# Graph attention with layer norm: empty rows found by DVE, additions and low parts moved to ACT and POOL, scores ahead of values, one store of turned weights

## The reference

```python
q, k, v = heads(x @ Wq.T), heads(x @ Wk.T), heads(x @ Wv.T)
a = einsum('bhnd,bhmd->bhnm', q, k) * 512 ** -0.5 + (adj + adj)[:, None]
row_nonzero = any(a != 0, axis=-1, keepdims=True)
a = where(row_nonzero, a, -inf)
p = softmax(a); p = where(isnan(p), 0.0, p)
o = einsum('bhnm,bhmd->bhnd', p, v)
out = layernorm(x + merge(o) @ Wo.T)
```

## Time and profile before

| | us |
|---|---|
| median of 3 runs | 2044.13 (2043.81 to 2044.32) |
| the profiled execution's own time | 2047.55 |
| its span | 2045.7 |
| PE busy | 1801.1 (88%) |
| DVE busy | 1605.2 (78%) |
| POOL busy | 1509.2 (74%) |
| ACT busy | 1228.8 (60%) |
| transfers of the SP queue | 378.61 MB, 69.5% of 16 DMA engines' span |

### The profile page before, as it was taken

The page is one execution under the profiler, slowest core; times in us unless marked ns, Lnnn a source line. Parts: engine busy times, 40 slices in busy tenths (PEclk is TensorE's granted clock), DMA queues, the critical chain, the costliest instruction groups (busy, mean ns, idle before and its releaser), DMA issues.

```text
span 2045.7 us, 46740 instructions
## 1 busy us (share of the span) xinstructions
PE 1801.1 (88%) x14370; PEld 1452.7 (71%) x14370; DVE 1605.2 (78%) x6191; ACT 1228.8 (60%) x4886; POOL 1509.2 (74%) x2292
## 2 busy tenths in 40 slices
PE   7798988989888999889889889898898989898886
PEld 5676777777776777767767777676776777777764
DVE  4887878878777878878878788787777887887786
ACT  5566566656655665566566656665665566556554
POOL 4567777777777777777777777777777777777765
PEclk9998998989999999999999899899998999999999
DMA  4667767777776677677767767777777777767664
GB/s 163 177 181 198 190 181 197 187 186 197 186 192 187 182 195 190 188 200 187 188 189 197 190 187 188 195 187 183 190 187 195 186 193 192 188 185 206 174 174 144
DMA packets 269290, 382.63 MB, mean 187 GB/s; under 512 B 19056, under 2 KB 149104, under 8 KB 268912
## 3 DMA queue, kind: packets, MB, share of 16 engines
q1 hardware_dynamic: 268464, 378.61, 69.5%
q10 hardware_dynamic: 576, 1.05, 0.1%
HBM read 212.86 MB, written 166.72 MB: 186 GB/s over the span
## 4 chain that ended last, share of the span: by engine, by line
POOL 43%; DMA 19%; DVE 15%; issue 10%; PE 7%; SPq 3%; ACT 1%; DVEq 0%; POOLq 0%; ACTq 0%
POOL is_zero L357 24%; DMA e_t<-blocks 15%; DVE neg_a L822 6%; POOL folded_once L360 4%; POOL xt_lo L347 4%; DVE e_sb L860 4%; DMA blocks<-e_b 3%; PE ps_s L535 3%; PE ps_o L553 3%; POOL folded_twice L362 3%; SPq L292 2%; POOL folded L367 2%; POOL ln_tmp L398 2%; DVE e_b L870 2%; DVE x_sb L798 1%
## 5 line engine op out<-in xcount | busy, mean ns | idle before, releaser
L690 ACT ACTIVATE e_sb<-neg_a,neg_max 128x128 f32<-128x128 f32 x2048 | 792.4, 392 | 71.3 <-DVE neg_max L822 70.9
L357 POOL TENSOR_SCALAR is_zero<-neg_a 128x1024 uint8<-128x1024 f32 x256 | 711.0, 2777 | 158.6 <-DVE neg_max L822 137.5
L676 ACT ACTIVATE x_sb<-x_sb,shift,rstd 128x512 f32<-128x512 f32 x124 | 100.9, 815 | 708.0 <-POOL shift L406 703.8
L822 DVE CUSTOM_DVE_ANT_0 neg_a<-ps_s,adj_sb 128x128 f32<-128x128 f32 x2048 | 441.7, 285 | 76.3 <-PE ps_s L535 76.3
L471 PE MATMUL ps_w<-xt_hi,w_lo 128*128 128x512 f32 x1020 | 426.6, 418 | 0.0
L472 PE MATMUL ps_w<-xt_lo,w_hi 128*128 128x512 f32 x1020 | 407.2, 399 | 0.0
L690 ACT ACTIVATION_READ_ACCUMULATOR e_sb<-neg_a,neg_max 128x1 f32 x2048 | 391.5, 191 | 0.0
L553 PE MATMUL ps_o<-e_t,v_sb 128*32 128x128 f32 x4080 | 167.3, 314 | 214.1 <-DMA e_t<-blocks 214.1
L870 DVE STREAM_TRANSPOSE e_b<-e_sb 128x1024 f32<-128x1024 f32 x254 | 316.3, 1245 | 27.0 <-DVE e_sb L860 0.5
L860 DVE SCALAR_TENSOR_TENSOR e_sb<-e_sb,r_inv 128x1024 f32<-128x1024 f32 x256 | 313.7, 1225 | 9.1 <-DVE r_inv L857 0.4
L553 PEld LDWEIGHTS ps_o<-e_t,v_sb 128*32 128x32 f32 x4080 | 128.0, 124 | 262.8 <-issue 261.2
(11 more groups left out here) (103 smaller groups left out, 2793.7 us busy)
## 6 DMA issues: line engine op xcount, KB each, us to landing
blocks<-e_b SPq DMA_DIRECT2D x254, 512.0 KB, 3.3
e_t<-blocks SPq DMA_DIRECT2D x508, 256.0 KB, 6.3
x_sb<-x SPq DMA_DIRECT2D x124, 256.0 KB, 5.3
out<-x_sb SPq DMA_DIRECT2D x124, 256.0 KB, 4.3
xt_raw<-xt SPq DMA_DIRECT2D x120, 256.0 KB, 5.3
adj_sb<-adj SPq DMA_DIRECT2D x32, 256.0 KB, 6.4
v_sb<-wk ACTq DMA_DIRECT2D x4, 256.0 KB, 6.7
neg_a<-xt SPq DMA_DIRECT2D x4, 256.0 KB, 6.0
```

Source lines behind the costliest of these rows:

```text
L357: pool.tensor_scalar(is_zero[:, :].bitcast(U8), rows, 0.0, None, ALU.is_equal).then_inc(zero_step, 1)
L676: act.activation(row, row, ACT.Identity, scale=rstd[:, i:i + 1], bias=shift[:, i:i + 1]).then_inc(normed, 1)
L690: last = act.activation(e_sb[:, i, h, :], neg_a[:, i, h, :], ACT.Exp, scale=-1.0, bias=neg_max[:, i, h:h + 1], accum_out=sums[:, i, h:h + 1])
L822: last = dve.tensor_tensor_reduce(out=neg_a[:, i, h, :], in0=ps_s[h][:, i * NODES:(i + 1) * NODES], in1=adj_sb[:, g % PAIR, i, :], scale=- ...
```

## The change

- **Empty rows.** `zeros` of POOL and L835 go. One DVE instruction (`smallest`) reduces neg_a to its largest value for each row, `largest` joins it with the row minimum to the largest absolute value, and `any_nonzero` asks once a phase whether that is above 0. bias of the next phase waits for abs_done in place of folded_done.
- **Addition and low parts.** ACT copies the output product out of its bank into y_sb, and POOL adds x; ACT copies the values out of ps_o into o_sb, and POOL makes the low part. PE gets both kinds of bank after ACT's copy. The last six graphs, and the last two phases, stay on DVE. To make room, o_hi and o_lo have one slot for tile 3 in place of two.
- **Order.** PE computes the scores of a phase ahead of the values. ACT makes the high part of the values after its first four exponentials in place of before them. ACT's normalisation, SP's store of a graph and its load of x come one phase later.
- **Store and move.** Both halves of e_b leave in one store of 1 MB, after the second transposition, in rows of 8 KB. The four moves now go by source block a, each to all 128 partitions.

The diff, cut to its core:

```diff
@@ sp @@
-            def save_blocks(f, half):
-                sp.wait_ge(transposed, 2 * f + half + 1)
-                sp.dma_start(blocks_d[f % 2, :, :, half], blocks_half[:, half]
-                             ).then_inc(saved[half], 16)
+            def save_blocks(f):
+                sp.wait_ge(transposed, 2 * f + 2)
+                sp.dma_start(blocks_d[f % 2], e_b[:, :].rearrange("p (b c) -> p b c", b=BLOCKS)).then_inc(saved, 16)
...
-                for b in range(BLOCKS):
-                    rows = slice(BLOCK * b, BLOCK * (b + 1))
-                    sp.dma_start(e_t[rows, :].rearrange("p (a c) -> p a c", a=BLOCKS),
-                                 blocks_d[f % 2, :, b].rearrange("(a j) m c -> j a (m c)", a=BLOCKS)
+                width = GG * TH * NODES // BLOCKS
+                for a in range(BLOCKS):
+                    rows = slice(BLOCK * a, BLOCK * (a + 1))
+                    sp.dma_start(e_t[:, width * a:width * (a + 1)], blocks_d[f % 2, rows].rearrange("j b c -> b j c")
                                  ).then_inc(moved, 16)
...
-                    save_blocks(f - 1, 1)
-                store(f - O_LAG - 2)
-                load_x(f - GG)
+                    save_blocks(f - 1)
+                store(f - O_LAG - 3)
+                load_x(f - O_LAG)
...
-                if f < LAST:
-                    save_blocks(f, 0)
@@ pool @@
+            def add(f, s):
...
+                    pool.wait_ge(o_copied, count("o", g, i))
+                    pool.tensor_tensor(row, y_sb[:, :], row, ALU.add).then_inc(added, 1)
+
+            def values_lo(f):
+                pool.wait_ge(values_copied, f + 1)
+                rest(o_lo[:, o_slot(f // TILES, f % TILES), :], o_sb[:, :], o_hi[:, o_slot(f // TILES, f % TILES), :]
+                     ).then_inc(o_lo_done, 1)
...
+                if f:
+                    add(f - 1, -1)
                 chunk_lo(window_chunk(f))
-                zeros(f, 0)
-                zeros(f, 1)
+                if f > 1:
+                    values_lo(f - 2)
@@ pe @@
             for f in range(LAST):
+                scores(f)
                 if f > 1:
                     values(f - 2, range(GG), ps_o)
-                scores(f)
@@ act @@
+                if kind == "o":
+                    if g or index:
+                        act.wait_ge(added, count(kind, g, index) - 1)
+                    copy(y_sb[:, :], in_).then_inc(o_copied, 1)
...
+                if f < LAST - 1:
+                    if f:
+                        act.wait_ge(o_lo_done, f)
+                    act.wait_ge(o_hi_done, f + 1)
+                    copy(o_sb[:, :], ps_o[:, :]).then_inc(values_copied, 1)
...
-                if f > 1:
-                    values_hi(f - 2)
+                if f and slots(f - 1)[-1][0] == "o":
+                    take(f - 1, -1)
...
                     exps(f, i)
                     if i % 2:
                         take(f, i // 2)
+                    elif i == 0 and f > 1:
+                        values_hi(f - 2)
@@ dve @@
+            def smallest(f):
+                dve.wait_ge(biased, GG * (f + 1))
+                dve.tensor_reduce(neg_min[:, :].rearrange("p a b -> p (a b)"),
+                                  neg_a[:, :].rearrange("p a b c -> p (a b) c"), AX.X, ALU.max).then_inc(min_done, 1)
+
+            def largest(f):
...
+                dve.scalar_tensor_tensor(out=abs_max[:, :], in0=neg_max[:, :], scalar=-1.0, in1=neg_min[:, :],
+                                         op0=ALU.mult, op1=ALU.max).then_inc(abs_done, 1)
...
             for f in range(PHASES):
-                if f:
-                    add(f - 1, -1)
                 bias(f)
+                smallest(f)
+                reciprocals(f, 0)
+                largest(f)
+                if f:
+                    stats(f - 1, -1)
+                any_nonzero(f)
+                if f:
+                    means(f - 1, -1)
+                row_factors(f, 0)
...
-                for half in range(2):
-                    any_nonzero(f, half)
-                    reciprocals(f, half)
-                    normalise(f, half)
-                    if f < LAST:
-                        turn_blocks(f, half)
+                normalise(f, 0)
+                if f < LAST:
+                    turn_blocks(f, 0)
...
+                reciprocals(f, 1)
+                row_factors(f, 1)
+                normalise(f, 1)
+                if f < LAST:
+                    turn_blocks(f, 1)
@@ DRAM @@
-    blocks = nc.dram_tensor("blocks", [2, P, BLOCKS, 2, 2 * TH * BLOCK], F32, kind="Internal").ap()
+    blocks = nc.dram_tensor("blocks", [2, P, BLOCKS, 2 * 2 * TH * BLOCK], F32, kind="Internal").ap()
```

More of the change, by code:

```diff
@@ L88, in o_slot @@
 def o_slot(g, tile):
-    return tile + TILES * (g % PAIR)
+    return tile + TILES * (g % PAIR) if tile < TILES - 1 else tile
 def window_chunk(f):
@@ L143, in build @@
         neg_max = sb("neg_max", [P, GG, TH])
[L144 to L148, removed]
+        neg_min = sb("neg_min", [P, GG, TH])
+        abs_max = sb("abs_max", [P, GG, TH])
         sums = sb("sums", [P, GG, TH])
@@ L196, in build @@
         biased = sem("biased")
-        zero_step = sem("zero_step")
-        folded_done = sem("folded_done")
         min_done = sem("min_done")
+        abs_done = sem("abs_done")
         exp_done = sem("exp_done")
         transposed = sem("transposed")
-        saved = [sem(f"saved{half}") for half in range(2)]
+        saved = sem("saved")
         moved = sem("moved")
@@ L323, in _ @@
                     sp.dma_start(v_sb[:, 1 - (GROUPS - 1) % PAIR], x_d[GROUPS - 1]).then_inc(last_x_loaded, 16)
-                if f < LAST:
-                    save_blocks(f, 0)
-            for n in range(LAST - O_LAG - 1, GRAPHS):
+            load_x(PHASES - O_LAG)
+            for n in range(LAST - O_LAG - 2, GRAPHS):
                 store(n)
@@ L701, in values_hi @@
                 g, t = f // TILES, f % TILES
-                if g > 1:
+                if t == TILES - 1 and g:
+                    act.wait_ge(made["o"], GG * g)
+                elif g > 1:
                     act.wait_ge(made["o"], GG * (g - 1))
@@ L797, in add, with stats @@
                 dve.wait_ge(made["o"], n)
-                dve.tensor_tensor(row, product_bank(kind, g, i)[:, :], row, ALU.add).then_inc(added, 1)
-            def moments(f, s):
+                dve.tensor_tensor(row, product_bank(kind, g, i)[:, :], row, ALU.add).then_inc(last_added, 1)
+            def stats(f, s):
                 todo = slots(f)
@@ L805, in moments @@
                 n = count(kind, g, i)
-                dve.wait_ge(added, n)
+                if n > LATE_O:
+                    dve.wait_ge(last_added, n - LATE_O)
+                else:
+                    dve.wait_ge(added, n)
                 if n > 2:
@@ L809, in moments, with means @@
                 dve.bn_stats(ln_stats[:, i % 2], x_row(g, i)).then_inc(stats_done, 1)
-                dve.wait_ge(stats_done, n)
+            def means(f, s):
+                todo = slots(f)
+                if not -len(todo) <= s < len(todo) or todo[s][0] != "o":
+                    return
+                kind, g, i = todo[s]
+                dve.wait_ge(stats_done, count(kind, g, i))
                 dve.bn_aggr((last_mean_var if g == GROUPS - 1 else mean_var)[:, i, :], ln_stats[:, i % 2]).then_inc(mean_done, 1)
```

132 lines of the change are left out of this document (65 added, 67 removed).

## The result

The changed kernel takes 2104.41 us (median of 4 runs, 2097.64 to 2105.37), the kernel before, run beside it, 2043.97 us (2037.56 to 2044.32): ratio 1.0296, 95% interval 1.0267 to 1.0326. It is 3% slower; 12% had been forecast, so the sign is right and the size is four times too large. The profiled execution has a span of 2103.6 us at a mean granted clock of 0.93.

A forecast was written before the change was run, and what follows sets the result against it. Four DMA engines carrying the moves were taken to bound the kernel: moves 11.9, store 3.0 and other transfers 2.7 us make 17.6 a phase against 15.59, over 125 phases 2295 us. The 8 in 10 range was 1755 to 2850 us.

The forecast's parts named there:

- What bounded before: Kernel before: late e_t transfers and POOL's chain, in a round over two phases of 31.2 us.
- Number of engines: Moves: their outermost loop of 4 puts them on four DMA engines, packets under 512 B near 10900.
- The sum closes the phase: SP's queue: moves, store and other transfers follow one another, 11.9, 3.0 and 2.7 us, 17.6 us a phase.
- the price of the moves: Moves of a phase: 1.05 MB on four engines at 22 GB/s each, 11.9 us.
- A's own range: Forecast case, four engines that run nearly freely: 16.6 to 21.7 us a phase, 2170 to 2810 us; chance 0.42.
- The store's term: Single store of 1.05 MB at 354 GB/s on sixteen engines: 3.0 us of the phase.
- rival E: Moves on four engines at over 25 GB/s, gap hidden: 15.4 to 15.7 us a phase, 2020 to 2058 us; chance 0.02.
- Rival B: Moves on four engines that slow one another: 13.1 GB/s each, 25.7 us a phase, 3308 us, in part from 2810; chance 0.17.
- Rival C: Moves on sixteen engines, PE bounds: 13.4 us a phase, 1770 us, with small waits up to 1845; chance 0.35.
- Rival D: Moves on sixteen engines, but a new wait at ACT, POOL or DVE of 1 to 2 us: 1908 to 2033 us; chance 0.04.
- DVE's work: DVE's new phase: 13.1 us in all, with 2.3 for the reduction, just under PE's 13.33.
- The sign named for it: Profile after, if four engines carry the moves: the chain that ended last runs through DMA e_t for over half.

The follow-up runs named there:

- ab_zp: The changed kernel with moves cut by destination rows again and POOL finding the empty rows again, without DVE's reduction: 2040.33 us, ratio 0.9967.
- b_sf: The kernel before with one edit, scores ahead of values: 2016.56 us, ratio 0.9879.
- a_b: The changed kernel with its four moves cut by destination rows again, 32 outermost rows at both ends: 1756.55 us, ratio 0.8596.
- a_dbl: The changed kernel, moves as changed, with two buffers of e_t and some tiles shared to make room: 2108.82 us, ratio 1.0333.
- a_late: The changed kernel with SP's other transfers of a phase issued behind the moves instead of between store and moves: 2404.6 us, ratio 1.1739.
- a_half: The changed kernel with each move cut in two, each with an outermost loop of 2 at the source: 3465.98 us in one run.

## Why the prediction was right or wrong

**What bounded before**: right. Two chains, DMA's to e_t and POOL's folds: with POOL's left in, the rest of the change gains 0.3% (ab_zp) and the order alone 1.2% (b_sf); with both relieved it is 14% (a_b).

**Number of engines**: right, and to the packet. "Near 10900" was foretold, 10928 came. The mean DMA share fell from 69.5% to 50.1% while DMA bounds, as it said. **The sum closes the phase**: right. a_dbl (no gain from a second buffer), a_late (the gap no longer filled, 2.4 us more) and a_half (nearly one to one) show it.

**The step that failed is the price of the moves, "I take 22 GB/s ... 11.9 us".** An engine carried 25.6 GB/s, and the moves took 10.3 us. That is above even the best bound, 24.0, so A's own range began too high as well. The rows behind the bounds were rates of sixteen engines together, divided by sixteen, and the forecast took the middle of two of them for an engine's own rate. Two and four engines at work carry 25.6 each (51 and 102 GB/s), and so do sixteen when twelve of them have the store's 8 KB rows and four the moves (409). So the reason given for going above 19.9, that a quarter of the engines crowds the memory less, is not shown: sixteen can have that rate too. The store's term has the same error: 3.0 us at 354 GB/s, where a sixteenth of it at 25.6 GB/s takes 2.6. Its pieces grew from 1 KB (the 149104 - 19056 = 254 x 512 packets of the earlier trace rows) to 8 KB, and this had not been priced. With 10.3 + 2.6 + 2.7 = 15.6 the sum would have given 2045; the measured phase is 16.05, so some 0.5 us of gap is left in it, which the prediction's sum had at nothing. If the other transfers too went at 409 GB/s, they would take 2.1 us and the gap would be 1.1; no window separates the two. The result lies between rival E (up to 15.7 us) and A's lower end (16.6 us): neither band held it, only the wide range over both signs did. E's rate, over 25 GB/s, is the one that came; its hidden gap is not.

The forecast was this sensitive because the phase before, 15.59, stands so near the sum: an error of 1.6 us in 17.6, 9%, is 195 us, over three times the whole effect. One more number of the prediction doesn't come out of its rows: values and scores at half the clock give PE 13.33 + 0.53 + 0.92 = 14.8 us, not 15.2. As PE is hidden in the sum, nothing hung on it.

**Rival B**, engines that slow one another on rows 32 apart: refuted. If the loop is what is shared out, the four engines write rows j, 32 + j, 64 + j and 96 + j, and they kept 25.6 GB/s each. So did two in a_half, 32 rows apart as well, and all sixteen together carried no more each. The Trainium skill, "SBUF — State Buffer", section on the DMA port swizzle, gives rows 32 apart one port; no run here shows that two engines on such rows slow each other. That 32-row moves over sixteen engines land later than 128-row ones (5.9 against 4.3 to 4.5 us) may belong to it; that is not shown. **Rival C**, sixteen engines: its time, 1770, is what a_b gives (1756.55). It is 13 us lower, mostly since the first values come at 45.63 us in a_b and at 56.38 before; the ends had been taken as equal. Its 13.4 us a phase is 13.36 there. **Rival D**, new waits of ACT or POOL: none reaches PE in a_b, which is busy 99.7% of the window.

**DVE's work**: the reduction was put at 2.3 us and took 2.286. Its phase was summed to 13.1; the window of a_b has 58.95 / 64 x 13.36 = 12.3, so the small instructions had been put too high (`nonzero` takes 0.16 us there, not 0.48), without effect, as PE bounds. The order at no cost and POOL below 60%: right (44%).

**Foretold in the profile and not so**: PEclk under 0.9 (it was 0.93) and a wait of 2 us or more in every phase (55 waits in some 62 phases, 2.2 on average, some under 1). The chain of the kernel after covers under 10% of its span and can't be read. The sign named for it, over half through DMA e_t, was probably wrong in itself: in a_half, where the chain is whole, e_t has 3%, and the chain runs through the landing of the store (49%) and the issuing of the moves (41%). A transfer that holds its engines shows there as the wait of what stands behind it. The landing time of the moves, "well over 12 us", can't be checked, as no page gives it.

**Not settled**: what makes up the last 0.5 us of the phase, and whether a permutation of v's rows would give the 128-row move for nothing; that was not tried.

## What to carry to other kernels

Read the outermost loop of both sides of every transfer. Here a loop of 4 put all moves on the same four engines and a loop of 2 on two, and everything behind them on the queue waited for these. The mean DMA share doesn't show it; the count of closing packets (16 for each transfer, or fewer) and a flat stretch at a small multiple of 25.6 GB/s do. And price an engine by the best stretch in which it is surely full, with the size of the pieces in mind: a mean rate divided by sixteen was only a lower bound here for what few engines do.

## What the runs showed that was not expected

- A DMA engine carried 25.6 GB/s with 2 or 4 at work in pieces of 2 KB (51, 102 GB/s), and with all 16 at work, twelve in pieces of 8 KB and four in pieces of 2 KB (409). Sixteen together on smaller pieces stayed below it before, 13.1 to 24.0 each; what of that is the size and what the number, no run separates.
- Eight moves on two engines took SP 12.47 us to issue in a_half, four moves on four engines 2.47 in the kernel after.
- The 32-row moves take 5.9 us to land and 128-row moves of the same bytes 4.3 to 4.5, both on sixteen engines.
- A STREAM_TRANSPOSE of 128x1024 whose input is read with a step of four takes 2038 ns against 1245; a score matmul whose moving operand has that step 408 ns on average against 283.
- The place of 0.85 MB of unrelated transfers on the queue, ahead of the moves or behind them, is worth 300 us of 2104.
